# Two more formed heads, even heads moved to ScalarE and VectorE, and attending that reads its high halves first

## The chip, the cores and the metric

The kernel runs on one core of a Trainium2 chip. Its time is the device time of one execution in microseconds; a shown time is the median of several runs. A core has a matrix engine (TensorE, PE), whose weight loads stand apart in the profile as PEld, and VectorE (DVE), ScalarE (ACT) and GpSimd (POOL). SyncE (SP) issues most DMAs. The engines run side by side and meet at semaphores.

## The reference

A block of attention and a mixture of low-rank experts, on x of 2 x 512 tokens of 512 values, in float32. There are 32 heads of 128.

```
x = x + layernorm(attention(layernorm(x)))
x = x + layernorm(ffn(layernorm(x)))

attention(n):
    q = rms_norm(n @ Wq + bq, gq)        # Wq, Wk, Wv: 512 x 4096; rms over all 4096 columns
    k = rms_norm(n @ Wk + bk, gk)
    v = n @ Wv + bv
    per head and batch: softmax(q k^T / sqrt(128)) v
    return concat(heads) @ Wo + bo       # Wo: 4096 x 512

ffn(n):
    base = n @ W_base.T + b_base
    g = softmax(n @ W_gate.T) - sigmoid(n @ W_thr.T + b_thr) / 8, cut at 0 and normed
    return base + 2 * sum over 8 experts e of g[e] * ((n @ A[e].T) @ B[e].T)
```

## The kernel before

**Precision.** A float32 operand is scaled and split into a float16 high half and a float16 low half. A product is three matmuls: high with high, high with low, low with high (lines 1857 to 1859). So every operand is made twice: the high half by ScalarE, the low half (value less high half) by VectorE or GpSimd.

**Stages.** First x is normed, transposed and split (0 to 25 us). Then stage A makes queries and keys of all heads, two heads a pair, 16 pairs, and stores them to a scratch tensor in HBM (to about 340 us). Then stage B attends: for each of 64 steps (16 pairs, 2 heads, 2 batches) the scores, the softmax, its turning by transposing DMAs, the product with the values and that with Wo. Then comes the ffn (from about 1000 us).

**A normal head in stage A** (`phase_a` on each engine) has four items g: query and key of batch 0, query and key of batch 1. An item is 12 matmuls of 128x512 (4 chunks of the contraction, 3 products) into one of eight PSUM banks, 0 to 3 for even heads and 4 to 7 for odd ones. Around it:

- ScalarE: the high halves of the weights of head h + 2, four squares (for the rms sums), and for each query two copies: float32 into `q_s` (line 1272) and the float16 high half into `qk_out` (line 1274).
- VectorE: the factors of head h + 2, the low halves of its weights (line 2550), the largest values of later weights, and the keys (`store_k`, line 2666), each after ScalarE's square of the same bank.
- GpSimd: the low half of each query, `q_s` less its high half (`low_q`, line 824), and adding the squares to `acc` (line 833), 8 additions a pair.
- SyncE: loads of weights, and the stores of a head's query and key, after VectorE's key and GpSimd's low half.

**A formed pair** has a normal even head and a formed odd head. A formed head makes query and key together from 7 products (W_C, W_A, W_E, W_B, W_D, W_G, W_F) of block sums of the weights with block sums of x, in place of 8 block products. Each of the 7 is 6 matmuls of 128x512: 2 chunks, 3 products (lines 1980 to 1982). The even head of a formed pair is already divided in another way: ScalarE makes the high half of the query, then its negated copy in `q_s` from it (line 1396), and the key too (line 1402); VectorE makes the low half from the PSUM bank and `q_s` (line 2799). The weight sums of a formed head are made by GpSimd (`formed_sums`, lines 908 and 913), their high halves by ScalarE (lines 1315, 1318), their low halves by VectorE (lines 2558, 2562). PE's product W_C waits for line 2562.

Pairs 8 to 14 are formed (`FIRST = PAIRS // 2`, `LAST_PAIR = PAIRS - 2`): seven formed heads. The last pair is a normal one.

**Block sums of x.** Four kinds (A, E, D by GpSimd, G by VectorE) are needed once, before the formed pairs. GpSimd's 22 operations on them (sums and low halves, line 850) lie between its additions, at most two kinds for each head of pairs 1 to 7; ScalarE casts the high halves (line 1327).

**Order.** Each engine's order is written out by hand, in the code. Waits are on counts of semaphores. PE's normal heads 2 to 13 are a loop in which the counts come from a register; heads 14 and 15 are written out.

**Attending** (`attend`, line 2090 on): for each of four blocks k three matmuls, value high with turned high, value high with turned low, value low with turned high, after both transposes have landed (lines 717 and 721 issue them, high first). The very last one (lines 2303, 2307) already reads all high halves first, and waits for the low ones after that.

## Time and profile before

| what | value |
|---|---|
| median of 3 runs | 1055.68 us (1052.35 to 1055.7) |
| the profiled execution | 1054.04 us |
| its span | 1052.1 us, 18937 instructions |
| PE busy | 1031.0 us (98%) |
| DVE, ACT, POOL busy | 869.5 (83%), 785.1 (75%), 779.1 us (74%) |

The span is from the first to the last instruction of the profiled execution; 1.9 us lie around it. Busy is the union of an engine's instructions. A matmul's end is modelled, so that matmuls overlap in the record; their starts tell the pace. A wait is named by what ended last before it.

### The profile page before, as it was taken

What the parts mean: (1) busy time and instruction counts of PE and PEld (TensorE: products, weight loads), DVE (VectorE), ACT (ScalarE), POOL (GpSimd) and SP (SyncE); (2) the same over time, 40 slices, a digit from 0 to 9 for tenths busy, and PEclk for the clock granted to TensorE, in tenths of its full rate; (3) what the DMA queues carried; (4) which work ended last, traced back from release to release, by engine and by line L of the source; (5) the groups of instructions that cost most, each with busy time, mean ns of one, the idle gap of its engine ahead of it and who ended that gap; (6) DMA issues with size and microseconds to landing.
All of it is one profiled execution on the core that took longest, in us unless ns stands there. A gap on an engine that the chain in (4) does not pass through costs nothing.

```text
span 1052.1 us, 18937 instructions
## 1 busy us (share of the span) xinstructions
PE 1031.0 (98%) x5607; PEld 544.9 (52%) x5607; DVE 869.5 (83%) x1883; ACT 785.1 (75%) x1618; POOL 779.1 (74%) x717
## 2 busy tenths in 40 slices
PE   7999999999999999999999999999999999999997
PEld 4444444444445655566555555555555555555454
DVE  8988988899886788777887987787887888888887
ACT  4775767777876787776787787788787788778656
POOL 2699999998986568775777877878778778667313
PEclk9999999999999999999999999999999999999999
DMA  6567755666655579958677777867857887886812
GB/s 243 190 228 268 255 201 194 234 243 217 216 189 183 141 190 288 226 134 207 144 194 193 175 181 189 172 171 193 202 161 171 215 192 168 207 200 141 176 36 81
DMA packets 308692, 200.04 MB, mean 190 GB/s; under 512 B 271472, under 2 KB 275440, under 8 KB 308592
## 3 DMA queue, kind: packets, MB, share of 16 engines
q1 hardware_dynamic: 304208, 194.24, 67.0%
q10 hardware_dynamic: 4384, 4.62, 1.6%
q8 instruction: 45, 0.74, 0.3%
q14 instruction: 55, 0.45, 0.1%
HBM read 96.03 MB, written 35.68 MB: 125 GB/s over the span
## 4 chain that ended last, share of the span: by engine, by line
PE 73%; DVE 12%; ACT 7%; issue 4%; DMA 1%; POOL 1%; SPq 1%; ACTq 0%; DVEq 0%; POOLq 0%
PE ps L1857 21%; PE ps L1858 21%; PE ps L1859 21%; PE ps L2120 3%; PE ps L2121 3%; PE ps L2122 3%; DVE pair_q L2960 2%; ACT ps L1537 2%; DVE wa_lo L2550 1%; DVE y L2973 1%; DMA pair_k<-pair_q 1%; ACT pair_q L1546 1%; ACT squares L1265 1%; DVE ps L2946 1%; PE ps L1980 1%
## 5 line engine op out<-in xcount | busy, mean ns | idle before, releaser
L2960 DVE SCALAR_TENSOR_TENSOR pair_q<-ps,row_inv,pair_q 128x512 f16<-128x512 f32 x256 | 174.4, 743 | 47.2 <-ACT pair_q L1546 43.4
L1537 ACT ACTIVATE ps<-ps,neg_max 128x512 f32<-128x512 f32 x256 | 168.3, 657 | 58.2 <-DVE ps L2946 58.2
L2946 DVE TENSOR_SCALAR_CACHE_REDUCE ps<-ps,score_down 128x512 f32<-128x512 f32 x256 | 177.2, 754 | 16.3 <-PE ps L1859 15.6
L1546 ACT ACTIVATE pair_q<-ps,row_inv 128x512 f16<-128x512 f32 x256 | 154.5, 689 | 7.3 <-DVE row_inv L2953 7.1
L1857 PE MATMUL ps<-xh,wa_hi 128*128 128x512 f16 x400 | 151.6, 379 | 1.8 <-DVE wa_lo L2550 1.8
L1859 PE MATMUL ps<-xh,wa_lo 128*128 128x512 f16 x400 | 151.6, 379 | 0.0
L1858 PE MATMUL ps<-xl,wa_hi 128*128 128x512 f16 x400 | 151.6, 379 | 0.0
L1018 POOL TENSOR_TENSOR k_lo<-qk_in,k_hi 128x512 f16<-128x512 f32 x62 | 71.7, 1157 | 39.3 <-ACT k_hi L1494 39.2
L1857 PE MATMUL ps<-wo_hi,oth 128*128 128x512 f16 x256 | 97.1, 379 | 1.2 <-issue 0.9
L1857 PE MATMUL ps<-k_hi,qk_in 128*128 128x512 f16 x256 | 97.1, 379 | 1.0 <-issue 0.7
L1858 PE MATMUL ps<-k_lo,qk_in 128*128 128x512 f16 x256 | 97.0, 379 | 0.0
L1859 PE MATMUL ps<-k_hi,qk_in 128*128 128x512 f16 x256 | 97.0, 379 | 0.0
L1859 PE MATMUL ps<-wo_hi,otl 128*128 128x512 f16 x256 | 97.0, 379 | 0.0
L1858 PE MATMUL ps<-wo_lo,oth 128*128 128x512 f16 x256 | 97.0, 379 | 0.0
L1049 POOL CAST oth<-o_t 128x512 f16<-128x512 f32 x62 | 38.4, 619 | 70.1 <-ACT o_t L1511 70.1
L1265 ACT ACTIVATE squares<-ps,q_k_bias,qk_down 128x512 f32<-128x512 f32 x100 | 77.5, 782 | 15.1 <-PE ps L1859 9.0
L1511 ACT ACTIVATE o_t<-ps,tab 128x512 f32<-128x512 f32 x62 | 42.7, 689 | 60.0 <-PE ps L1859 59.8
L833 POOL TENSOR_TENSOR acc<-acc,squares 128x512 f32<-128x512 f32 x64 | 85.1, 1350 | 0.0
L1012 POOL TENSOR_TENSOR qk_in<-qk_in,rms_row 128x512 f32<-128x512 f32 x62 | 78.9, 1272 | 0.6 <-ACT rms_row L1499 0.6
L924 POOL TENSOR_TENSOR acc<-acc,squares 128x512 f32<-128x512 f32 x56 | 75.0, 1364 | 0.6 <-ACT squares L1265 0.5
L1051 POOL TENSOR_TENSOR otl<-o_t,oth 128x512 f16<-128x512 f32 x62 | 71.6, 1155 | 5.0
L2973 DVE SCALAR_TENSOR_TENSOR y<-ps,y_down,y 128x1024 f32<-128x1024 f32 x55 | 70.1, 1274 | 0.0
(373 smaller groups left out, 2785.3 us busy)
## 6 DMA issues: line engine op xcount, KB each, us to landing
q_k_scratch<-qk_out SPq DMA_DIRECT2D x64, 512.0 KB, 3.0
qk_in<-q_k_scratch SPq DMA_DIRECT2D x64, 512.0 KB, 3.7
wa_stage<-w_qk SPq DMA_DIRECT2D x32, 512.0 KB, 4.4
u_stage<-w_vo SPq DMA_DIRECT2D x32, 512.0 KB, 5.2
wo_stage<-w_vo SPq DMA_DIRECT2D x16, 512.0 KB, 6.4
x_first<-w_vo SPq DMA_DIRECT2D x12, 512.0 KB, 4.6
qk_tops<-qk_top_scratch ACTq DMA_DIRECT2D x27, 128.0 KB, 3.9
pair_k<-pair_q SPq DMA_TRANSPOSE x130, 4.0
```

Of the source, the lines that this page charges most:

```text
L833: pool.tensor_tensor(acc[:, w, cols], acc[:, w, cols], squares[:, par, w, cols], ALU.add).then_inc(acc_ready, 1)
L924: pool.tensor_tensor(part(acc[:, w, :]), part(acc[:, w, :]), part(squares[:, par, w, :]), ALU.add).then_inc(acc_ready, 1)
L1012: pool.tensor_tensor(qk_in[:, s, 0, :], qk_in[:, s, 0, :], factors(b), ALU.mult).then_inc(qk_scaled, 1)
L1265: act.activation(squares[:, par, w, b * S:(b + 1) * S], ps[:, 4 * par + g, :], ACT.Square, bias=q_k_bias[:, par, w:w + 1], scale=qk_down[: ...
L1537: act.activation(ps[:, SCORE + i, :], ps[:, SCORE + i, :], ACT.Exp, bias=neg_max[:, sl, i:i + 1], scale=-1.0, accum_out=row_sum[:, sl, i:i ...
L1546: act.activation(pair_q[:, 0, i, :], ps[:, SCORE + i, :], ACT.Identity, scale=row_inv[:, sl, i:i + 1]).then_inc(high_ready, 1)
L1857: pe.matmul(outp, lhs[0], rhs[0], start=first, stop=False)
L1858: pe.matmul(outp, lhs[0], rhs[1], start=False, stop=False)
L1859: return pe.matmul(outp, lhs[1], rhs[0], start=False, stop=last)
L2946: dve.tensor_scalar(ps[:, SCORE + i, :], ps[:, SCORE + i, :], score_down[:, sl, i:i + 1], None, ALU.mult, ALU.min, accum_out=neg_max[:, sl ...
L2960: dve.scalar_tensor_tensor(out=pair_q[:, 1, i, :], in0=ps[:, SCORE + i, :], scalar=row_inv[:, sl, i:i + 1], in1=pair_q[:, 0, i, :], op0=AL ...
L2973: dve.scalar_tensor_tensor(out=y[:, tiles, :], in0=ps[:, YB:YB + 2, :], scalar=y_down[:, :], in1=y[:, tiles, :], op0=ALU.mult, op1=ALU.add ...
```

## The change

- `FIRST` becomes `PAIRS // 2 - 2`: pairs 6 to 14 are formed, nine formed heads, and pairs 1 to 5 are normal ones of the new kind.
- Even heads of normal pairs 1 to 5 are divided between ScalarE (`even_head`) and VectorE (`even_low`) as in a formed pair; GpSimd's `low_q` goes for them, and SyncE's stores wait for VectorE's low half.
- GpSimd's sums of x go six to a pair into pairs 1, 2 and 3, the rest into 4 and 5.
- PE waits, before an even head writes a query bank, for VectorE's low half of the even head before. PE's loop is written out.
- `attend` runs its 8 matmuls with turned high halves first, and waits for the low transpose only before the other 4.

```diff
-        FIRST, LAST_PAIR = PAIRS // 2, PAIRS - 2
+        FIRST, LAST_PAIR = PAIRS // 2 - 2, PAIRS - 2
...
-        X_FORMS, X_CASTS, Q_LOWS = 22, 8, 2 * FORMED_A
+        X_FORMS, X_CASTS, Q_LOWS = 22, 8, 2 * LAST_PAIR
...
+            def store_even(h, b):
+
+                sp.wait_ge(k_out_ready, 2 * h + 1 + b)
+                sp.wait_ge(k_low_ready, h - 1 + b)
+                sp.dma_start(q_k_scratch[h:h + 1, b].rearrange("a p w n -> p (a w) n"),
+                             qk_out[:, 0, b]).then_inc(stored[0][b], 16)
...
@@ GpSimd
-                        low_q(par, b, 2 * h + b + 1)
+                        if par:
+                            low_q(par, b, 2 * h + b + 1)
...
-            phase_a(1, high_a, low_a)
-            phase_a(2, both_halves)
-            phase_a(3, split_a, high_e)
-            phase_a(4, low_e)
-            phase_a(5, split_e, high_d)
-            phase_a(6, low_d, split_g)
-            for p in range(7, FIRST):
-                if p == FIRST - 1:
-                    formed_sums(2 * FIRST + 1)
-                if p == 7:
-                    phase_a(p, split_d)
-                else:
-                    phase_a(p)
+            phase_a(1, high_a, low_a, both_halves)
+            phase_a(2, split_a, high_e, low_e)
+            phase_a(3, split_e, high_d, low_d)
+            phase_a(4, split_d)
+            formed_sums(2 * FIRST + 1)
+            phase_a(5, split_g)
...
@@ ScalarE
+            def even_head(h, slot, cast):
+
+                for b in range(2):
+                    half = slice(b * S, (b + 1) * S)
+                    act.wait_ge(acc_ready, 4 * h + 2 + 2 * b)
+                    act.wait_ge(stored[0][b], 8 * h)
+                    act.wait_ge(qk_product, 4 * h + 2 * b + 1)
+                    act.activation(pair(qk_out[:, 0, b, 1, :])[:, 0, :], ps[:, 2 * b, :], ACT.Identity,
+                                   bias=q_b[:, slot:slot + 1], scale=Q_DOWN)
+                    square(0, 2 * b, slot, 4 * h + 2 * b + 1)
+                    if b == 0:
+                        load_tops(h + 3, 1)
+                        act.wait_ge(k_out_ready, 2 * h)
+                        act.wait_ge(k_cols_ready, 3 * h + 3)
+                    act.wait_ge(sq_ready, 4 * h + 2 * b + 1)
+                    act.activation(q_s[:, 0, half], pair(qk_out[:, 0, b, 1, :])[:, 0, :], ACT.Identity,
+                                   bias=q_b[:, slot:slot + 1], scale=-1.0).then_inc(q_hi_ready, 1)
+                    square(0, 2 * b + 1, slot, 4 * h + 2 * b + 2)
+                    act.activation(qk_out[:, 0, b, 0, :], ps[:, 2 * b + 1, :], ACT.Identity,
+                                   bias=gain_up[:, h:h + 1], scale=k_g[:, slot:slot + 1]).then_inc(k_out_ready, 1)
+                    if b == 0:
+                        store_tops(h + 4, 0)
+                        if cast is not None:
+                            cast_x(cast, 0)
...
-            casts = {3: XA, 5: XE, 6: XG, 7: XD}
+            casts = {2: XA, 3: XE, 4: XD, 5: XG}
...
@@ TensorE
                 pe.wait_ge(k_out_ready, 2 * h - 3)
+                if par == 0 and h > 2:
+                    pe.wait_ge(k_low_ready, h - 3)
                 q_or_k(par, 0, o % 4)
...
-            with pe.Fori(1, PAIRS // 4) as i:
-                for o in range(-2, 2):
-                    phase_a(i, o)
-            for i, o in NORMAL[14:]:
+            for i, o in NORMAL[2:]:
                 phase_a(i, o)
...
             def attend(n, sl, b, bank=OB, v=(vh, vl)):
                 pe.wait_ge(high_turned, 16 * n + 16)
-                pe.wait_ge(low_turned, 16 * n + 16)
                 d = slice(sl * P, (sl + 1) * P)
                 for k in range(TB):
-                    ins = three(ps[:, bank, :], (v[0][:, TB * b + k, d], v[1][:, TB * b + k, d]),
-                                (pair_k[:, sl, 0, :, k, :], pair_k[:, sl, 1, :, k, :]), k == 0, k == TB - 1)
+                    for half in range(2):
+                        pe.matmul(ps[:, bank, :], v[half][:, TB * b + k, d], pair_k[:, sl, 0, :, k, :],
+                                  start=k == 0 and half == 0, stop=False)
+                pe.wait_ge(low_turned, 16 * n + 16)
+                for k in range(TB):
+                    ins = pe.matmul(ps[:, bank, :], v[0][:, TB * b + k, d], pair_k[:, sl, 1, :, k, :],
+                                    start=False, stop=k == TB - 1)
                 ins.then_inc(o_product, 1)
...
@@ VectorE
+            def even_low(h, b):
+
+                dve.wait_ge(q_hi_ready, 2 * h + 1 + b)
+                dve.scalar_tensor_tensor(out=pair(qk_out[:, 0, b, 1, :])[:, 1, :], in0=ps[:, 2 * b, :],
+                                         scalar=Q_DOWN, in1=q_s[:, 0, b * S:(b + 1) * S], op0=ALU.mult,
+                                         op1=ALU.add).then_inc(k_low_ready, 1)
+
...
                 for b in range(2):
-                    dve.sem_inc(begun, 1)
-                    dve.wait_ge(stored[par][b], 16 * (2 * i + o // 2))
-                    dve.sem_inc(begun, 1)
-                    store_k(par, b, o % 4, 4 * h + 2 * b + 2)
+                    if par:
+                        dve.wait_ge(stored[par][b], 16 * (2 * i + o // 2))
+                        store_k(par, b, o % 4, 4 * h + 2 * b + 2)
+                    else:
+                        even_low(h, b)
```

## Rows read from the trace of the kernel before

**Rows 1.** The page: busy times by engine, PE clock by slice, chain by engine.
```profile
PE 1031.0 (98%) x5607; PEld 544.9 (52%) x5607; DVE 869.5 (83%) x1883; ACT 785.1 (75%) x1618; POOL 779.1 (74%) x717
...
PE 73%; DVE 12%; ACT 7%; issue 4%; DMA 1%; POOL 1%; SPq 1%; ACTq 0%; DVEq 0%; POOLq 0%
```

**Rows 2.** Chain of waits in order of time: start us, us, what.
```profile
789.26 0.22 PE ps L1858
...
968.63 2.04 ACT ps L1537 x6
...
977.61 2.04 ACT ps L1537 x6
...
991.33 6.07 DMA pair_k<-pair_q
```

**Rows 3.** Timeline of PE, product W_C: start us, us, engine line op [idle before].
```profile
205.71 0.38 PE L1980 MATMUL ps<-xh,rms_row 128*128 128x512 f16 x1
...
225.13 0.38 PE L1980 MATMUL ps<-xh,w_form_a 128*128 128x512 f16 x1
...
244.77 0.39 PE L1980 MATMUL ps<-xh,rms_row 128*128 128x512 f16 x1
...
284.39 0.39 PE L1980 MATMUL ps<-xh,rms_row 128*128 128x512 f16 x1
...
303.66 0.38 PE L1859 MATMUL ps<-xh,wa_lo 128*128 128x512 f16 x1
304.37 0.39 PE L1980 MATMUL ps<-xh,w_form_a 128*128 128x512 f16 x1 [0.33 <-DVE w_form_a L2562]
```

**Rows 4.** Table of stretches: stretch, its us, busy us (instructions) by engine, clock, DMA.
```profile
225.13:244.77 19.64, 19.59 (x92) 8.73 (x90) 17.40 (x34) 15.64 (x27) 17.06 (x15) 1.00 0.64 232
...
284.39:304.37 19.98, 19.65 (x91) 8.61 (x91) 17.76 (x34) 15.89 (x27) 17.40 (x15) 1.00 0.55 198
...
59.00:79.70 20.70, 20.70 (x98) 9.39 (x97) 17.96 (x33) 15.09 (x26) 20.62 (x17) 1.00 0.66 228
```

**Rows 5.** Timeline of DVE, key of a formed head and what it waited for.
```profile
286.13 0.81 DVE L2793 TENSOR_SCALAR qk_out<-ps,k_b,k_g 128x512 f32<-128x512 f32 x1 [1.20 <-ACT squares L1373]
```

**Rows 6.** Instructions on `qk_out`: count, duration ns min/median/max, first and last start.
```profile
L824 POOL TENSOR_TENSOR qk_out<-q_s,qk_out x36: 1146/1158/1610, 28.6 to 381.7; 128x512 f16<-128x512 f32 x36
...
L1396 ACT ACTIVATE q_s<-qk_out,q_b x14: 710/712/723, 188.5 to 318.2; 128x512 f32<-128x512 f16 x14
L1402 ACT ACTIVATE qk_out<-ps,gain_up,k_g x14: 762/766/772, 192.4 to 322.2; 128x512 f32<-128x512 f32 x14
L2799 DVE SCALAR_TENSOR_TENSOR qk_out<-ps,q_s x14: 674/678/684, 194.5 to 322.1; 128x512 f16<-128x512 f32 x14
```

**Rows 7.** Timeline of ACT, a cast of a sum of x.
```profile
161.29 0.64 ACT L1327 ACTIVATE xs<-qk_in 128x512 f16<-128x512 f32 x1
```

**Rows 8.** Timelines of POOL (additions of head 3) and ACT (square of head 5).
```profile
64.66 2.95 POOL L833 TENSOR_TENSOR acc<-acc,squares 128x512 f32<-128x512 f32 x2
...
77.70 0.78 ACT L1265 ACTIVATE squares<-ps,q_k_bias,qk_down 128x512 f32<-128x512 f32 x1 [0.46 <-PE ps L1859]
```

**Rows 9.** Timeline of PE before attends, and its row in the list of waits.
```profile
907.58 0.27 PE L2122 MATMUL ps<-w_form_b,xl 128*128 128x256 f16 x1
907.92 0.38 PE L1857 MATMUL ps<-pair_k,v_b 128*128 128x512 f16 x1
...
980.08 0.38 PE L1859 MATMUL ps<-wo_hi,otl 128*128 128x512 f16 x1
980.72 0.38 PE L1857 MATMUL ps<-pair_k,v_b 128*128 128x512 f16 x1 [0.26 <-DMA pair_k<-pair_q]
...
995.20 0.38 PE L1859 MATMUL ps<-wo_hi,otl 128*128 128x512 f16 x1
997.44 0.39 PE L2303 MATMUL ps<-pair_k,v_b 128*128 128x512 f16 x1 [1.86 <-DMA pair_k<-pair_q]
...
PE ps L1857 <- DMA pair_k<-pair_q: 0.8, 3, 0.3
```

More of the change, by code:

```diff
@@ L553, in store_qk, with store_half @@
                              qk_out[:, par, b]).then_inc(stored[par][b], 16)
+            def store_even(h, b):
[3 more added lines that the diff above has]
+                             qk_out[:, 0, b]).then_inc(stored[0][b], 16)
+            def store_half(h, b):
+                if h % 2 == 0:
+                    store_even(h, b)
+                else:
+                    store_qk(h, 1, b, 2 * h + 1 + b, h - 1)
             def phase_a(i, o, weights=True, unit=3, more=None):
@@ L627, in formed_pair @@
                 sp.wait_ge(k_out_ready, 2 * h + 4)
-                sp.wait_ge(q_lo_ready, 4 * FIRST + 2 * f + 2)
+                sp.wait_ge(q_lo_ready, h + 4)
                 for b in range(2):
@@ L895, in split_g @@
             def split_g(c):
-                low_half(XG, two(qk_in[:, 2, c, :]), c, 5 + c)
+                low_half(XG, two(qk_in[:, 2, c, :]), c, 7 + c)
             def split_d(c):
-                low_half(XD, of_first(c), c, 7 + c)
+                low_half(XD, of_first(c), c, 5 + c)
             def formed_sums(h):
@@ L1325, in cast_x @@
                 else:
-                    act.wait_ge(x_formed, {XA: 5, XE: 11, XD: 18}[kind] + c * (2 if kind == XD else 1))
+                    act.wait_ge(x_formed, {XA: 3 + 3 * c, XE: 9 + 3 * c, XD: 15 + 3 * c}[kind])
                 act.activation(xs[:, 0, kind, c, :], qk_in[:, 2 if kind == XG else 0, c, :],
                                ACT.Copy).then_inc(k_high_ready, 1)
+            def even_head(h, slot, cast):
[21 more added lines that the diff above has]
+                            cast_x(cast, 0)
             def phase_a(i, o, formed=False, cast=None):
@@ L1341, in phase_a @@
                 act.wait_ge(q_b_ready, h + 1)
+                if par == 0:
+                    even_head(h, o % 4, cast)
+                    return
                 for g in range(4):
@@ L1944, in phase_a @@
                 pe.wait_ge(k_out_ready, 2 * h - 1)
+                if par == 0 and h > 2:
+                    pe.wait_ge(k_low_ready, h - 2)
                 q_or_k(par, 2, o % 4)
@@ L2677, in _ @@
             dve.wait_ge(k_cols_ready, 6)
+            dve.scalar_tensor_tensor(out=gain_up[:, :], in0=tab[:, 1, :], scalar=X_UP, in1=tab[:, 3, :],
+                                     op0=ALU.mult, op1=ALU.mult)
             first_factors(2)
@@ L2745, in phase_a @@
                         largest_of_unit(h + more, (par + more) % 2, 16 * (2 * i + (o + more) // 2 + 1))
-            phase_a(1, -2, unit=0)
-            phase_a(1, -1, unit=0)
-            phase_a(1, 0, unit=0)
-            phase_a(1, 1, unit=0, more=1)
-            phase_a(2, -2, unit=1, more=2)
             def half_g(half, c, to):
@@ L2760, in both_g @@
                                   ALU.add).then_inc(x_by_dve, 1)
-            dve.wait_ge(xl_ready, NT)
-            half_g(xh, 0, 2)
-            phase_a(2, -1)
-            half_g(xl, 0, 3)
-            phase_a(2, 0)
-            half_g(xh, 1, 2)
-            phase_a(2, 1)
-            half_g(xl, 1, 3)
-            phase_a(3, -2)
-            both_g(0)
-            phase_a(3, -1)
-            both_g(1)
-            dve.scalar_tensor_tensor(out=gain_up[:, :], in0=tab[:, 1, :], scalar=X_UP, in1=tab[:, 3, :],
-                                     op0=ALU.mult, op1=ALU.mult)
-            for h in range(12, 2 * FIRST):
-                phase_a(*NORMAL[h], formed=h == 2 * FIRST - 1)
+            units = {2: (0, None), 3: (0, None), 4: (0, None), 5: (0, 1), 6: (1, 2)}
+            sums_of_g = {4: (half_g, xh, 0, 2), 5: (half_g, xl, 0, 3), 6: (half_g, xh, 1, 2),
+                         7: (half_g, xl, 1, 3), 8: (both_g, 0), 9: (both_g, 1)}
+            for h in range(2, 2 * FIRST):
+                unit, more = units.get(h, (2, None))
+                phase_a(*NORMAL[h], unit=unit, more=more, formed=h == 2 * FIRST - 1)
+                if h == 4:
+                    dve.wait_ge(xl_ready, NT)
+                if h in sums_of_g:
+                    one, *where = sums_of_g[h]
+                    one(*where)
             def formed_pair(p, more=None):
@@ L2794, in formed_key @@
                                       k_g[:, slots[1]:slots[1] + 1], ALU.add, ALU.mult).then_inc(k_out_ready, 1)
-                def even_low(b):
-                    dve.wait_ge(q_hi_ready, 2 * h + 1 + b)
-                    dve.scalar_tensor_tensor(out=pair(qk_out[:, 0, b, 1, :])[:, 1, :], in0=ps[:, 2 * b, :],
-                                             scalar=Q_DOWN, in1=q_s[:, 0, b * S:(b + 1) * S], op0=ALU.mult,
-                                             op1=ALU.add).then_inc(k_low_ready, 1)
                 next_factors(h + 2, 0, (h + 2) % 4)
@@ L2827, in formed_pair @@
                     low_wa(h + 3, (h + 3) % 4)
-                even_low(1)
+                even_low(h, 1)
                 formed_key(1, 8 * p + 8)
```

29 lines of the change are left out of this document (14 added, 15 removed).

## The prediction

> **What bounds the kernel now.** I read the page's busy shares first. TensorE (PE) is busy 98% of the span, every other engine 83% or less, and three quarters of the chain that ended last is PE [rows 1]. The PE clock digits are all 9 (full speed), so no clock is to be won. The reader is to see that only two things shorten this kernel: fewer PE instructions, or a PE idle stretch that goes and whose successor isn't late for another reason.
>
> Next the chain of waits in order of time, to see where that is not so [rows 2]. Up to about 880 us it is matmul after matmul. From there to the last step it is a ring of ScalarE exponentials (ACT), VectorE low halves (DVE) and transposing DMAs: one round from 968.63 to 977.61 is 8.98 us, without PE in it. It ends in a DMA of 6.07 us, for which PE waits before 997.44 [rows 9].
>
> Third, the matmuls in order of time. The page gives a 128x512 matmul 379 ns, but that is latency; what counts is the distance of starts. From the first product of one formed pair to that of the next it is 225.13 - 205.71 = 19.42 us [rows 3], over 90 matmuls (48 of the even head, 42 of the formed head): 0.2158 us each. I read the waits from starts too, since a gap under 0.16 us is hidden in the modelled ends.
>
> **What the change removes on PE.** A normal head is 4 items of 12 matmuls, 48. A formed head is 7 products of 6, 42. FIRST goes from 8 to 6, so pairs 6 and 7 become formed: 2 x 6 x 0.2158 = 2.6 us less PE work. A normal pair takes 96 x 0.2158 = 20.7 us, and the table of stretches shows PE without a gap over such a pair [rows 4].
>
> The Trainium skill ("TensorE: Matmul & The Clock Gate", section Back-to-back issue gap) gives about 131 ns a matmul of 512 columns in a sustained stream; by it the removed work would be an estimated 12 x 0.131 = 1.6 us. The same section's formula for a single one gives 216 ns, and that is what this case's starts show, so the measured 0.2158 is used.
>
> **What a formed pair really costs.** The next starts of that product are 244.77, 284.39 and 304.37 [rows 3]. So periods are 19.42, 19.64, then 39.62 for two, then 19.98 us: 0.2, 0.4 (twice), 0.5 above the 19.42 that PE needs. The later the pair, the more it waits. The wait is in front of this very product: from 303.66 to 304.37 is 0.71 instead of 0.22 us, and the row names DVE line 2562 (low halves of the formed weights). In the period to 304.37 DVE is busy 17.76 us [rows 4] and stands 1.20 us waiting for ACT's square before line 2793 [rows 5]; with some 0.2 us gaps between its small dependent factors it needs about 19.8 to 20 us a pair. DVE enters the formed stage with a lead, PE eats it in two pairs, and after that the DVE/ACT loop sets the pace. None of this loop is edited. So nine formed pairs in a row are two free ones and seven that wait, and the two added ones are of the waiting kind: 20.7 - 19.9 = 0.8 us gained each, **1.6 us** for both, not 2.6. The bounds are 2.6 (the lead lasts, periods 19.42) and 0.5 (the wait keeps growing by some 0.15 a pair, to 20.3 and 20.6: 0.4 + 0.1). I take the value nearest to the last period measured.
>
> **Even heads of pairs 1 to 5: ACT and DVE instead of POOL.** Per even head ACT keeps 4 squares and 2 query copies, swaps 2 for the negated copies (712 ns) and gets 2 keys (766 ns) [rows 6]: +1.6 us a pair. The stretch of a normal pair has ACT busy 15.09 of 20.70 us [rows 4]; it goes to 16.7, and with both casts of x (0.64 each [rows 7]) to at most 18. DVE gives up 2 keys of 0.81 (the same operation as in rows 5) and gets 2 low halves of 0.68: -0.3 us on 17.96. POOL loses 2 low halves of 1.16 [rows 6]. All this hides under the 20.7 us of PE: **0**. Below nothing isn't possible, since PE has no wait there. PE gets two new waits, for the low half of the head before last in the same bank; that was made a whole odd head (10.4 us) earlier, and behind it only PE's own items queue. ACT gets a wait for DVE's keys of the head before, which DVE makes ahead of the factors that ACT has waited for already, so nothing new is late. If this cover fails, what is late is the ring of the rival below. SP's stores of even heads no longer wait for POOL, so the loads queued behind them can only be earlier.
>
> **Sums of x, six a pair.** All 22 sums and splits must be done by pair 6 instead of pair 8. POOL in pair 1 had 4 low halves, 8 additions and 4 sums, 16 operations. Now pairs 1 to 3 have 2 + 8 + 6 = 16 each, pairs 4 and 5 have 12, with four weight sums between. At the pace of 16 in 20.6 us of POOL [rows 4] POOL keeps up with PE in pairs 1 to 3, but catches nothing up, as it could before in pairs 2 and 4 (14 operations). Its reserve: the additions that end at 67.61 free squares that ACT writes next at 77.70 [rows 8], about 10 us. After pair 5 the last split is due only when W_D begins, 60 matmuls or 13 us into pair 6. **0**, with an upper bound in the rival below. The other edits (one small DVE operation moved forward, PE's loop of 12 heads written out, counts of semaphores) have no row that waits for them: 0, at most 0.2 us each.
>
> **Attending reads high halves first.** The same 12 matmuls, with the 4 that read the low halves last, 8 x 0.216 = 1.7 us later. The low transpose is issued after the high one and lands later, so the wait for it shrinks by up to 1.7 us. Where did PE wait there? Four times; of them the first and the last stand in [rows 9]: 907.58 to 907.92 is 0.34 where a half-width matmul needs 0.11, and 980.08 to 980.72 is 0.64 where 0.22 is needed. All four come to 1.5 us by starts. The list of waits has three of them, 0.8 us, since it sees only what lies beyond the modelled ends. All four would go. But all lie after 900 us, where the chain runs through ACT, DVE and DMA [rows 2]. PE gets there sooner and then stands longer for the last transposes (995.20 + 0.22 to 997.44 is 2.0 us now; 3.5 then). I take 0.2 us of the 1.5, since the transposes wait for the attend before; bounds 0 and 1.5.
>
> **Sum.** 1.6 + 0 + 0 + 0.2 = 1.8 us. The profiled execution took 1054.04 us (span 1052.1 and 1.94 around it), 1.64 below the median shown, 1055.68, in runs from 1052.35. From the profile the sum gives 1052.2, from the median 1053.9; I name the middle, **1053.1 us**. A difference of 0.3% (3.2 us) is about what a measurement of this kernel can tell from no change, and the sum is 0.17%.
>
> **Rivals.**
> - Everything counts: DVE's lead lasts, so 2.6 us, and the ring behind 900 us is PE's after all, so 1.5 more. 4.1 us, 1050.8 from the same middle. For it: the first two periods of formed pairs are free, and some waits in the ring are near PE's own step. Against it: the growth of the wait, and 8.98 us of ring without PE. Chance 0.22.
> - The formed stage is worse: each later pair waits more, 20.3 and 20.6 us, gain 0.5 us, and the attend edit brings 0: 1054.4. For it the rising series. Against it: DVE's own work stays 17.4 to 17.8 us a pair. Chance 0.20.
> - Slower: POOL falls behind in pairs 1 to 3. Place: the additions that free the squares. The low halves take from 1.15 to 1.61 us [rows 6]; if all 16 took 1.60, a pair would be 25.6 us, 4.9 over PE's 20.7, 14.7 after three pairs, less 10 of reserve: 4.7 us on PE, net 2.9 slower, 1057.8. It decides from a mean of 1.50 us an operation (24 us a pair, 3.3 over, three times). The mean now is 20.62 / 16 = 1.29 [rows 4]. Chance 0.10. The Trainium skill ("SBUF — State Buffer", section SBUF: two separate sides) names a port pair that DVE operations with two SBUF inputs and GpSimd operations hold exclusively; here DVE's new low half reads PSUM and one SBUF input, so by that rule it would not add to it. No run here shows it.
> - That the change does not do what it says: the formed pairs count 9 but the waits move before the first of them. That is in the ranges above.
>
> **Numbers.** Forecast 0.48. Faster by over 0.3%: nearly all of the first rival and the upper edge of the forecast, 0.27. Slower: the last rival, 0.10. Same 0.63. The range reaches from just below the first rival, 1050.0, to 1056.5, short of the slow rival.
>
> **What would show it.** Right: matmuls fall by 12; formed pairs from about 142 us on (the first now begins at 205.71 - 102 x 0.2158 = 183.7, less two normal pairs of 20.7); periods 19.4, 19.4, then 19.6 to 20.0, total wait near 2.5 us; no PE wait in 38 to 142 us; POOL full until about 120 us; no wait before an attend, but a longer one before the last attend, line 2303 now. Wrong: a PE wait in pairs 1 to 5, periods that stay 19.42, or a last wait that does not grow.

## The result and the profile after

| | median us (runs) | profiled run, us | span | granted clock |
|---|---|---|---|---|
| before | 1053.08 (6) | 1054.04 | 1052.1 | 0.999 |
| after | 1057.92 (6) | 1056.82 | 1055.0 | 0.997 |

After / before is 1.004, with 0.9983 forecast; the 95% interval is 1.0027 to 1.0053. The change made the kernel slower by 4.2 us by that ratio (0.4%; the two medians differ by 4.8), and 1057.92 lies outside the range on record. One execution of e5 (3883.57 us) and one of e7 (2819.38 us) below were far slower than all others, and the ratios go by the fast runs alone. The two profiled runs differ by less, 2.8 us. The forecast of 1053.1 also started too high, since the three runs first shown (median 1055.68) lay above the later ones (1053.1 to 1053.7 in every set). By ratio it is off by 0.6%.

The page of the kernel after, the rows that answer to [rows 1]:

```profile
PE 1030.4 (98%) x5595; PEld 543.7 (52%) x5595; DVE 885.6 (84%) x1889; ACT 798.8 (76%) x1636; POOL 770.7 (73%) x711
...
PE 63%; DVE 15%; ACT 12%; issue 6%; DMA 2%; POOL 1%; ACTq 1%; SPq 1%; DVEq 0%; POOLq 0%
```

The busy shares say almost nothing: the 12 matmuls are gone, POOL is less busy, PE still at 98%. The chain says more: PE's part fell from 73% to 63%, and DVE, ACT and issue took it over. The view that settles it is the timeline of PE where the chain leaves PE (start us, us, engine line op, idle before and its releaser):

```profile
144.81 0.38 PE L1895 MATMUL ps<-xh,wa_lo 128*128 128x512 f16 x1
148.30 0.48 PE L2016 MATMUL ps<-xh,w_form_a 128*128 128x512 f16 x1 [3.12 <-DVE qk_out L2704]
148.57 0.63 PE L2017 MATMUL ps<-xl,w_form_a 128*128 128x512 f16 x1
149.00 0.63 PE L2018 MATMUL ps<-xh,w_form_a 128*128 128x512 f16 x1
...
151.56 0.53 PE L2018 MATMUL ps<-xs,wa_lo 128*128 128x512 f16 x1
151.93 0.38 PE L2016 MATMUL ps<-xs,wa_hi 128*128 128x512 f16 x1
```

From 144.81 to 148.30 is 3.49 us, where a matmul needs 0.22: a wait of 3.3 us in front of product W_C of the first formed pair. In this pair alone the code waits there for VectorE's first key of head 11 (batch 0). Behind it the starts are 0.43 apart until 151.56, twice 0.216. The table of stretches for these two windows (PEclk is the number behind POOL's count):

```profile
148.30:151.80 3.50, 3.50 (x9) 1.31 (x10) 2.29 (x5) 3.37 (x7) 3.50 (x4) 0.52 0.37 150
151.80:155.30 3.50, 3.50 (x17) 1.57 (x16) 3.08 (x10) 3.15 (x6) 3.50 (x4) 0.99 0.79 219
```

The granted clock is 0.52, the 1.2 GHz level, right behind the stand, then 0.99. Nine matmuls start in the first window and 17 in the second; by starts the nine took 1.7 us longer than at the upper level. (Whether these 1.7 us are a price of their own is looked at under e5.) The Trainium skill ("TensorE: Matmul & The Clock Gate", section Wait — 56ns, not 53.3ns?) gives starts of 426.7 ns at 1.2 GHz and 215.7 ns at 2.4 GHz for 512 columns; the trace agrees with both (0.43, 0.216).

Stage A, up to the first column sum, ends 2.9 us later: in before it starts at 334.22, in after here:

```profile
337.13 1.84 PE L2070 MATMUL ps<-ones,acc 128*128 128x1 f32 x16
```

The account by distances of starts: -2.6 (12 matmuls) + 3.3 + 1.7 + 0.4 (waits before later W_C and smaller ones, 2.0 in all against 1.6) + 0.2 (first 25 us) = 3.0, against the 2.9 read off. Two executions of the same code up to this point can differ too: e1 and e9 below, which change nothing in stage A, end it at 334.88 and 335.33. The rest of the span changes little in the profiled runs: from there to the start of the last matmul of the last attend (stage B) it is 665.6 us in before and 665.1 in after, behind it 52.3 and 52.8. Inside stage B something is hidden all the same, at the one backward branch of its loop. ACT and PE there, after:

```profile
682.99 0.69 ACT L1547 ACTIVATE o_t<-ps,tab 128x512 f32<-128x512 f32 x1 [2.25 <-issue]
```
```profile
683.00 0.39 PE L1893 MATMUL ps<-k_hi,qk_in 128*128 128x512 f16 x1 [1.38 <-issue]
```

("issue" is time in which the engine waited for nothing that the profile shows), and in before, where ACT waits for PE at that place and not for "issue":

```profile
679.00 0.39 PE L1857 MATMUL ps<-k_hi,qk_in 128*128 128x512 f16 x1 [0.70 <-issue]
```

### The profile page after: what moved, and what is told of

Its sections match the earlier page's. It is cut to its first block, busy times and chain, and to the rows that moved or that the text cites. A ratio compares the mean times of both kernels' runs of the same rounds, so it can differ in the third digit from the quotient of the medians.

```text
span 1055.0 us, 18786 instructions
## 1 busy us (share of the span) xinstructions
PE 1030.4 (98%) x5595; PEld 543.7 (52%) x5595; DVE 885.6 (84%) x1889; ACT 798.8 (76%) x1636; POOL 770.7 (73%) x711
## 4 chain that ended last, share of the span: by engine, by line
PE 63%; DVE 15%; ACT 12%; issue 6%; DMA 2%; POOL 1%; ACTq 1%; SPq 1%; DVEq 0%; POOLq 0%
PE ps L1893 13%; PE ps L1895 12%; PE ps L1894 12%; PE ps L2129 9%; PE ps L2133 4%; PE ps L2158 3%; PE ps L2160 3%; PE ps L2159 3%; ACT squares L1273 3%; ACT ps L1573 2%; DVE pair_q L2992 2%; DVE wa_lo L2588 2%; ACT wa_hi L1240 2%; DMA pair_k<-pair_q 1%; PE ps L2016 1%
## 5 line engine op out<-in xcount | busy, mean ns | idle before, releaser
L1893 PE MATMUL ps<-xh,wa_hi 128*128 128x512 f16 x368 | 139.5, 379 | 1.8 <-DVE wa_lo L2588 1.8
L1895 PE MATMUL ps<-xh,wa_lo 128*128 128x512 f16 x368 | 139.5, 379 | 0.0
L1894 PE MATMUL ps<-xl,wa_hi 128*128 128x512 f16 x368 | 139.5, 379 | 0.0
L1273 ACT ACTIVATE squares<-ps,q_k_bias,qk_down 128x512 f32<-128x512 f32 x92 | 71.3, 777 | 8.5 <-PE ps L1895 5.4
```

The source lines that it names most:

```text
L1273: act.activation(squares[:, par, w, b * S:(b + 1) * S], ps[:, 4 * par + g, :], ACT.Square, bias=q_k_bias[:, par, w:w + 1], scale=qk_down[: ...
L1893: pe.matmul(outp, lhs[0], rhs[0], start=first, stop=False)
L1894: pe.matmul(outp, lhs[0], rhs[1], start=False, stop=False)
L1895: return pe.matmul(outp, lhs[1], rhs[0], start=False, stop=last)
```

## Why the wait is there: a ring, not a sum

What ends the wait is DVE's first key of head 11 at 147.34; it waited for ACT's square at 146.42, and this for ACT's start into the head. ACT, after:

```profile
139.87 0.77 ACT L1356 ACTIVATE qk_out<-ps,gain_up,k_g 128x512 f32<-128x512 f32 x1
142.16 0.72 ACT L1323 ACTIVATE wa_hi<-wa_stage,qk_up 128x512 f16<-128x512 f32 x1 [1.53 <-DVE qk_up L2529]
...
146.42 0.79 ACT L1273 ACTIVATE squares<-ps,q_k_bias,qk_down 128x512 f32<-128x512 f32 x1
```

DVE, after:

```profile
139.33 0.69 DVE L2769 SCALAR_TENSOR_TENSOR qk_out<-ps,q_s 128x512 f16<-128x512 f32 x1 [1.35 <-ACT q_s L1353]
...
140.82 1.11 DVE L2571 TENSOR_SCALAR qk_down<-qk_most 128x2 f32<-128x2 f32 x1
141.97 0.17 DVE L2529 RECIPROCAL qk_up<-qk_down 128x2 f32<-128x2 f32 x1
...
147.34 0.81 DVE L2704 TENSOR_SCALAR qk_out<-ps,k_b,k_g 128x512 f32<-128x512 f32 x1 [0.90 <-ACT squares L1273]
```

ACT can't begin the weights of head h + 2 before DVE has their factors; DVE gets to the factors only behind its last key or low half of the head before; and that waits for ACT's squares and copies. Both engines stand in turns, each for the other: from 37.22 to 142.16 us ACT is busy 71% and DVE 85%, and where each waits for the other the ring still has no slack. In this ring the start of head 13's weights is at 142.16, where before had 135.81: 6.4 us later, while PE comes only 0.2 later. Against before ACT's starts were 1.8 us late at 37 us, 2.1 at 65, 4.7 at 100 and 6.4 at 142. Three places feed this.

1. At the start. The moved `gain_up` (in before it took 1.25 us behind head 11, at 145.47) and a pair of low weights that now takes 2.27 us (1.37 before) put ACT's first start in the ring at 37.22 instead of 35.38. DVE, after:

```profile
29.17 0.84 DVE L2716 SCALAR_TENSOR_TENSOR gain_up<-tab 128x32 f32<-128x32 f32 x1
...
34.52 2.27 DVE L2588 SCALAR_TENSOR_TENSOR wa_lo<-wa_stage,qk_up,wa_hi 128x512 f16<-128x512 f32 x2
```

2. Heads 5 and 6. DVE's six operations for kind G of the block sums of x (tile XG) stand behind the last key or low half of heads 4 to 9, where before had them at the same place of heads 6 to 11. With the second `largest_of_unit` they now share heads 5 and 6; in before they shared only head 6. DVE and, in the second fence, ACT, after:

```profile
84.03 1.21 DVE L2712 TENSOR_REDUCE vo_top<-u_stage 128x1 f32<-128x1024 f32 x1
85.15 1.69 DVE L2798 TENSOR_TENSOR qk_in<-xl 128x512 f32<-128x512 f16 x1
...
96.22 1.21 DVE L2712 TENSOR_REDUCE vo_top<-u_stage 128x1 f32<-128x1024 f32 x1
97.35 1.57 DVE L2798 TENSOR_TENSOR qk_in<-xh 128x512 f32<-128x512 f16 x1
```
```profile
75.77 1.33 ACT L1240 ACTIVATE wa_hi<-wa_stage,qk_up 128x512 f16<-128x512 f32 x2 [1.27 <-DVE qk_up L2529]
87.83 1.33 ACT L1240 ACTIVATE wa_hi<-wa_stage,qk_up 128x512 f16<-128x512 f32 x2 [4.64 <-DVE qk_up L2529]
99.90 1.34 ACT L1240 ACTIVATE wa_hi<-wa_stage,qk_up 128x512 f16<-128x512 f32 x2 [2.99 <-DVE qk_up L2529]
```

ACT's starts are 12.06 and 12.07 us apart there, a head of PE is 10.4. In before the ring was over PE's pace at this place too, but less, 11.2 and 11.1 us (72.81, 84.02, 95.16), so each of the two heads adds 0.9 us to the lag:

```profile
84.02 1.34 ACT L1232 ACTIVATE wa_hi<-wa_stage,qk_up 128x512 f16<-128x512 f32 x2 [2.95 <-DVE qk_up L2491]
95.16 1.33 ACT L1232 ACTIVATE wa_hi<-wa_stage,qk_up 128x512 f16<-128x512 f32 x2 [3.69 <-DVE qk_up L2491]
```

3. The cast of x (0.64 us), now in each of heads 4 to 11; before had only four of the eight by 142 us.

The shares of the three were not taken apart.

PE doesn't feel the lag in normal heads: they need the key of the head before only with their third item, 24 matmuls in. The first formed pair asks for it 12 matmuls in, and begins at head 12 instead of 16.

## The experiments

Every run was timed in five rounds beside the kernel before, whose medians were 1053.74 (e1 to e4), 1053.18 (e5 to e8), 1053.12 (e9 to e11) and 1053.43 (e12). Changes are told by ratio.

| run | median us (runs) | ratio to before, 95% | stage A ends | stage B |
|---|---|---|---|---|
| e1 attend alone | 1053.92 (11) | 1.0001 (0.9992 to 1.0011) | 334.88 | 664.5 |
| e2 formed from pair 8 | 1056.80 (8) | 1.0029 (1.0018 to 1.0039) | 332.94 | 669.3 |
| e3 XG sums beside | 1053.28 (11) | 0.9999 (0.9990 to 1.0008) | 332.88 | 666.1 |
| e4 key item first | 1057.28 (5) | 1.0041 (1.0027 to 1.0055) | 337.10 | 666.1 |
| e5 after, loop written out | 1054.66 (11) | 1.0020 (1.0009 to 1.0031) | 337.41 | 663.6 |
| e6 e2, loop written out | 1050.51 (11) | 0.9974 (0.9965 to 0.9983) | 333.44 | 662.3 |
| e7 e3 and casts earlier | 1053.41 (11) | 1.0006 (0.9996 to 1.0016) | 333.57 | 665.2 |
| e8 e7, loop written out | 1050.35 (11) | 0.9976 (0.9967 to 0.9985) | 334.28 | 663.0 |
| e9 before, loop written out | 1053.08 (11) | 0.9999 (0.9990 to 1.0008) | 335.33 | 665.5 |
| e10 e3, loop written out | 1051.60 (11) | 0.9976 (0.9961 to 0.9991) | 333.11 | 663.2 |
| e11 e6 with XG sums beside | 1051.36 (11) | 0.9982 (0.9972 to 0.9992) | 332.77 | 662.9 |
| e12 e2 and 16 idle instructions | 1051.88 (12) | 0.9983 (0.9973 to 0.9993) | 332.84 | 664.3 |

**e1: the kernel before with the new order of attending alone.**

```diff
                 pe.wait_ge(high_turned, 16 * n + 16)
-                pe.wait_ge(low_turned, 16 * n + 16)
...
+                pe.wait_ge(low_turned, 16 * n + 16)
```

The rest of the edit is the order of the twelve matmuls, as in the change.

> The kernel before with only the new order in attend. Ring theory (the time is lost in stage A, before the first formed head): the four waits before attends go (1.5 us in the trace of before), the wait for the last transposes grows by as much, the time is that of before within 1 us. Rival, the new attend costs something by itself (more PE waits or a later ring of ACT and DVE in stage B): slower by 1 to 3 us. Rival of my forecast's upper side: faster by 1.5 us.

1.0001: the attend edit brings nothing and costs nothing that can be told.

**e2: the changed kernel, formed pairs from pair 8 on.** As before the change, seven formed heads.

```diff
-        FIRST, LAST_PAIR = PAIRS // 2 - 2, PAIRS - 2
+        FIRST, LAST_PAIR = PAIRS // 2 - 0, PAIRS - 2
```

GpSimd's part gets the two further normal pairs, with the weight sums ahead of the last one.

> The changed kernel with pairs 8 to 14 formed as before (seven formed heads); even heads of pairs 1 to 7 divided in the new way, sums of x six a pair, new attend. Ring theory: ACT and DVE are as late at head 11 as in the changed kernel (ACT begins the weights of head 13 near 142 us), but have two pairs without casts and sums of x to catch up, so no PE wait before the first product W_C and no fall of the clock; 1052 to 1054 us, as before. Rival, the new division of even heads or the sums of x cost PE time by themselves: a PE wait between 38 and 184 us, slower by 2 us or more. Rival, GpSimd is late: it is busy without a gap up to 142 us and ACT waits for acc.

The wait before the first formed pair is gone, and so are the small ones in front of the later W_C (0.1 us in all by starts). ACT's lag near 142 us is as in after (141.17 for head 13), so it takes both to make PE stand: the lag, and a formed stage that begins before it is made up. Stage A ends at 332.94, 1.3 us ahead of before, with 12 matmuls more than after. The time missed what I expected (1052 to 1054): it was hardly better than after, since stage B is 4.2 us longer than in after, 3.7 longer than in before. DVE of e2 at the loop's branch:

```profile
680.02 0.76 DVE L2983 TENSOR_SCALAR_CACHE_REDUCE ps<-ps,score_down 128x512 f32<-128x512 f32 x1
684.61 0.08 DVE L2983 DVE_READ_ACCUMULATOR ps<-ps,score_down 128x1 f32 x1 [3.83 <-issue]
```

```profile
683.97 0.38 PE L1900 MATMUL ps<-wo_hi,otl 128*128 128x512 f16 x1
687.89 0.28 PE L2163 MATMUL ps<-w_form_b,xh 128*128 128x256 f16 x1 [3.54 <-ACT ps L1601]
...
688.55 0.42 PE L2164 MATMUL ps<-w_form_b,xh 128*128 128x256 f16 x1
688.77 0.42 PE L2165 MATMUL ps<-w_form_b,xl 128*128 128x256 f16 x1
```

DVE stands in the middle of its own row of instructions, waiting for no semaphore that the profile shows. This was the first sign of a second cause.

**e3: the sums for XG moved off the ring**, behind the first unit of the head instead of behind its last key or low half (shortened):

```diff
                     if b == 0:
                         largest_of_unit(h + unit, ...)
+                        if h in sums_of_g:
+                            one(*where)
...
-                if h in sums_of_g:
-                    one(*where)
```

> The changed kernel with VectorE's six operations for the sums of kind G moved from the end of heads 4 to 9 (between its last key or low half and the factors of head h + 2, for which ScalarE waits) to the middle of the same head (after the first largest_of_unit), where it waits 1.0 to 1.8 us for ScalarE. Same work. Ring theory: each such head is 1 to 1.5 us shorter in the ring, ScalarE begins the weights of head 13 at 137 to 139 us instead of 142.2, the PE wait of 3.3 us before the first W_C goes or falls below 1 us, the clock keeps its upper level, gain 3.5 to 5 us against the changed kernel: 1053 to 1054.5. Rival, VectorE's total of work binds and not its order: nothing changes, 1058. Rival, the wait comes from the weight sums (GpSimd, ScalarE line 1326) and not from the keys of head 11: nothing changes.

Stage A of e3 against after, PE in front of the first formed pair and at the column sum:

```profile
144.85 0.38 PE L1895 MATMUL ps<-xh,wa_lo 128*128 128x512 f16 x1
145.06 0.38 PE L2016 MATMUL ps<-xh,w_form_a 128*128 128x512 f16 x1
...
332.88 1.84 PE L2070 MATMUL ps<-ones,acc 128*128 128x1 f32 x16
```

No wait, no fall of the clock, ACT's start of head 13's weights at 136.84 instead of 142.16, stage A 4.2 us shorter than in after and 1.3 shorter than in before. The same six operations, done on the same engine at another place in its order, win back the whole loss of stage A. It is not DVE's total of work: from 75.5 to 99.6 us DVE is busy 22.21 us here, and in after from 75.77 to 99.90 only 20.95. Since before had the six at the end of heads too, only two heads later, this shows how the time is lost, and not that they alone made the lag.

**e4: the first formed pair's key item put in front of W_C.**

```diff
                 q_or_k(0, 0, slots[0])
+                if f == 0:
+                    q_or_k(0, 1, slots[0])
                 pe.wait_ge(wa_lo_ready, 2 * h + 4)
```

The item's old place goes for this pair, and two of ACT's counts follow the new order.

> The changed kernel with one reorder in the first formed pair alone: PE does the key of batch 0 of the even head (12 matmuls, 2.6 us) before product W_C. Ring theory: the PE wait is 3.3 - 2.6 = 0.7 us and stands before W_C as before, the clock does not fall, gain 4 us: 1053.5 to 1054.5. Rival, PE's wait is for something that comes after PE's own order (a buffer that the later items free): the wait stays 3 us. Rival, the clock falls for another reason than the wait: the half pace stays, gain 2.6 us.

A miss of my expectation: W_C starts at 148.29 as in after, and 2.6 us of other work ahead of it only moved the wait behind W_A, in front of W_E, with the fall of the clock behind that. PE of e4:

```profile
148.29 0.38 PE L2016 MATMUL ps<-xh,w_form_a 128*128 128x512 f16 x1 [0.53 <-DVE qk_out L2707]
...
153.90 0.59 PE L2016 MATMUL ps<-xs,w_form_a 128*128 128x512 f16 x1 [2.86 <-ACT ps L1405]
```

ACT's copy L1405, for which W_E waits, starts at 153.17, and at 153.18 in after, where PE comes to W_E only later. So it is ACT as a whole that is late, not one key, and of the two cures only e3's is one.

**e5: the changed kernel with stage B's loop written out** on all five engines.

```diff
-            with pe.Fori(1, FORMED // 2) as i:
+            for i in range(1, FORMED // 2):
```

> The changed kernel with the loop of stage B written out on all five engines (its one backward branch lies near 680 us; there the profile has ScalarE stand 2.2 us and PE 1.4 us for nothing that it shows). Same work and order. Theory that part of the loss is this branch, whose price depends on where the change has moved the code: stage A ends at 337.1 us as before, the stands near 680 us go, stage B is 0.6 to 1.5 us shorter, 1056.5 to 1057.3. Rival, the stands are waits on other engines that the profile doesn't name: they stay. Rival, more code costs fetches: slower.

The stands at the branch are gone, the 3.3 us before the first formed pair stay (145.10 to 148.61). 1.0020 against 1.0040: about 2 us are the branch's, by ratios whose intervals just overlap (1.0009 to 1.0031, 1.0027 to 1.0053). By the profiles it is 1.5 us of stage B. All eight profiled kernels with the loop have PE stand for "issue" there, 0.54 to 0.81 us in before, e1, e2 and e12, and 1.34 to 1.88 in after, e3, e4 and e7, where ACT also stands 2.1 to 2.6. None of the six with the loop written out has such a stand there.

This run also tells what the fall of the clock was worth. Behind the same stand of 3.3 us the clock stayed at its upper level (a row of PE's timeline and the same stretch as above, both of e5):

```profile
148.61 0.38 PE L2016 MATMUL ps<-xh,w_form_a 128*128 128x512 f16 x1 [3.12 <-DVE qk_out L2704]
...
148.30:151.80 3.50, 3.19 (x15) 1.49 (x16) 2.42 (x4) 3.47 (x7) 3.50 (x4) 1.00 0.37 150
```

But stage A is no shorter. From the matmul behind the last transposes of x (25.61 us in after, 25.89 here) to the column sum it is 311.52 us in both. PE came sooner and stood instead: 0.4 us for ACT's copy L1405 at 154.21, and 0.2, 0.3 and 0.6 before the next three W_C, where after has next to nothing. So the end of stage A was set by DVE and ACT, and the 1.7 us of the lower clock in after lie where PE would have waited anyway.

**e6: e2 with the loop written out.**

> The kernel of e2_eight_first (pairs 8 to 14 formed) with stage B's loop written out. In e2 VectorE stood 3.8 us at 680.8 us for nothing shown, PE waited 3.5 us after it, and the clock was at its lower level for some 4 us. Branch theory: all of it goes, 3.7 + 2 = 5.7 us less, 1051 us, the fastest so far, with no PE wait in stage A. Rival, the new division or the six sums a pair cost the 3 us of e2 by themselves: 1056 to 1057.

0.9974, as the branch theory says: no PE wait in stage A, no stand at the branch, and stage B is 662.3 us, 7.0 less than in e2.

**e7: e3, and the casts of x moved to the start of a head on ACT.**

```diff
                 h, par = 4 * i + o, o % 2
+                if cast is not None:
+                    cast_x(cast, par)
```

> e3_g_beside and with it ScalarE's eight casts of the sums of x moved from the middle of a head to its start, ahead of the high halves of weights, where ScalarE waits 1.3 to 3.3 us for VectorE's factors. Ring theory: each head with a cast is up to 0.5 us shorter in the ring, ScalarE begins the weights of head 13 at 133 to 135 us (142.2 in the changed kernel, 136.8 in e3), no PE wait before the first W_C, and stage A ends no later than in e3 (332.9 us). 1052 to 1053.5, as stage B decides. Rival, ScalarE's work is the bound and not its place in the ring: as e3, 136.8.

1.0006 against e3's 0.9999, and ACT starts the weights of head 13 at 136.93, as the rival says: the place of the casts doesn't matter.

**e8: e7 with the loop written out.**

> e7 with the loop of stage B written out. Both theories: stage A as in e7 (332.9 us or earlier), stage B without the stand at the branch, 664.5 us or less: 1050.5 to 1051.5 us, 2 to 3 us under the kernel before and the fastest of all. If the end of stage B is set by the ring of ScalarE, VectorE and transposes alone, only 1 us of it shows: 1052.

0.9976, with stage B at 663.0 us: as expected.

**e9: the kernel before with the loop written out**, the control for e5, e6, e8 and e10.

> The kernel before with the loop of stage B written out on all engines, nothing else. It tells how much of the 2.5 to 3 us that the two written-out versions of nine heads and of eight gained over the kernel before is only the loop's branch. Theory (the branch has a price that hangs on the layout of the code, and the kernel before pays the smallest one seen: its profile shows PE standing only 0.70 us near the branch, where the others show PE 1.4 to 3.7 and ACT or DVE 2.2 to 3.8): faster by 1 to 1.5 us, 1051.7 to 1052.3 against 1053.2, stage B 664.1 to 664.6 instead of 665.1. Then the change with its sums beside the ring and the loop written out (1050.4) keeps 1.3 to 1.9 us of its own, near the 1.6 of the prediction. Rival: the branch costs the kernel before as much as the others (3 us), 1050.3, and the whole gain of those versions is the branch, none the change's. Second rival: written-out code of this length costs something by itself (fetching), no gain.

Theory and first rival missed: 0.9999, the second rival's number. Whether the kernel before pays nothing at the branch, or written-out code costs as much as the branch saves, this run can't tell (its profile has no stand at the branch, but waits of 1.6 and 0.7 us at 517 and 527 us, for a transpose and for ACT, where the other profiles have none and at most 0.5; and the execution profiled was the slowest of the eleven). The 665.1 us that the text on record gives for stage B of the kernel before are those of after; before has 665.6, and e9 665.5. Either way it is the control: what e6, e8 and e10 have over it is the change's own and not the loop's. The branch cost after about 2 us and e2 about 6 (1.0029 to 0.9974).

**e10: e3 with the loop written out.**

> The changed kernel with the sums of gates moved off the ring of ScalarE and VectorE (as in the run with only that edit, 1053.3) and the loop of stage B written out. The casts stay at their place. Theory: both causes are gone at once, and they add: 1053.3 less the branch (3.3 us in the changed kernel, 6.3 in the one of eight heads; stage B should come to 662.3 to 663.6 from 666.1), so 1050.0 to 1050.8, as the version that also moves the casts (1050.4). Rival: the casts' place has a price that the branch hid, and this one is 0.5 to 1 us behind, 1051.1 or more.

0.9976, the same as e8 by ratio. By the medians of its set it is 0.9986, and its 1051.60 lies in the range of the rival; the interval (0.9961 to 0.9991) holds both, so the two theories are not told apart.

**e11: e6 with the XG sums beside the ring.** The text on record calls this eight formed heads; FIRST is pair 8 as in e2, so there are seven.

> As the run before it in this call, but with eight formed-or-later start (FIRST back at 8 heads' pairs less one: eight formed heads instead of nine), sums of gates beside the ring, loop written out. It tells what the ninth formed head is worth once both causes are gone. By the periods of the prediction a further formed pair that waits brings 0.8 us. Theory: with one formed pair less, the formed stage begins later, VectorE's lead is as large and PE does not wait in it, so the formed head that is left out costs nothing on the clock: equal to the nine-head version within 0.5 us, 1050.0 to 1050.8. Rival: the ninth head brings its 6 matmuls and more, 1.3 us, and this one is at 1051.5.

0.9982 with seven formed heads, 0.9976 with nine: the two heads on which the forecast counted 1.6 us bring at most a few tenths, and the intervals overlap. Table of stretches, PE busy first, of e11 and then of e10 over their formed pairs:

```profile
184.00:303.00 119.00, 119.00 (x554) 53.93 (x552) 103.48 (x200) 95.38 (x155) 99.30 (x83) 1.00 0.62 214
```
```profile
203.80:303.10 99.30, 98.32 (x451) 43.17 (x450) 88.62 (x166) 79.90 (x132) 87.33 (x71) 1.00 0.63 220
```

With seven PE never stands, with nine it stands 1.0 us beyond the modelled ends (2.4 us by starts), which takes back nearly all of the 2.6 us of matmuls. This is as the theory on record has it.

**e12: e2 with 16 semaphore additions on DVE in front of its loop**, which nobody waits for.

```diff
+            for _ in range(16):
+                dve.sem_inc(begun, 1)
             with dve.Fori(1, FORMED // 2) as i:
```

> The version with seven formed heads (formed pairs from pair 8 on, as before the change) and the loop of stage B kept, plus 16 semaphore additions that nobody waits for, on VectorE alone, just ahead of its loop. Without them this version took 1056.8 (1.0029 times the kernel before), and its VectorE stands 3.83 us near 684 us at the loop's branch, with TensorE 3.7 behind it. Theory (the price hangs on where the loop's code lies, not on what the code does): VectorE's stand changes by more than 1 us, to 0 to 2.5, stage B falls from 669.3 to 664 to 667, and the time to 0.998 to 1.001 of the kernel before, 1051 to 1054. ScalarE or TensorE may show a stand of its own, 1 to 2.5, that lay under VectorE's. Rival: the stand belongs to the work at that place (the same loop in all versions, entered with this version's order of the buffers), the shift of code does nothing, VectorE 3.8 again and 1056.8. Second rival: the position within the code decides, but 16 instructions are a whole number of its blocks, and nothing changes; then this run can't tell it from the first rival.

From 1.0029 to 0.9983, 4.9 us faster by 16 instructions that do nothing. DVE of e12 at the place where e2 stood 3.83 us:

```profile
680.64 0.76 DVE L2983 TENSOR_SCALAR_CACHE_REDUCE ps<-ps,score_down 128x512 f32<-128x512 f32 x1
681.31 0.14 DVE L2983 DVE_READ_ACCUMULATOR ps<-ps,score_down 128x1 f32 x1
```

Neither the loop nor its work differ from e2, only where DVE's code lies. The additions themselves cost nothing: DVE's rows ahead of them (512.88 us) and behind them (521.84) are both 0.2 us later than in e2. Of e2's stands there only PE's own is left (0.81 us). So the price at the branch hangs on where the code lies; one shift on one engine was tried. What moves there can be seen in the DMA queues of the stretch 675 to 690 us (packets, MB, share), here of after; before, e2 and e12 have seven or eight such packets there too, e5 has none, e6 one and e9 two:

```profile
q8 instruction: 3, 0.05, 1.8%
q14 instruction: 5, 0.04, 0.8%
```

The Trainium skill ("Runtime: NRT & Kernel Launch", section Instruction fetch mechanics) says that a taken branch whose target isn't in the small window of code at hand stops the engine until it is fetched, and that code comes in blocks of 256 instructions. The traces agree with the first: stands and seven or eight packets of code at the branch in the looped kernels, no stand and at most two packets without it. The block size no run here shows.

## Why the prediction was wrong, step by step

- **Matmuls, 12 fewer, 0.2158 us each: right.** 5607 to 5595.
- **Formed pairs, -1.6 us for two more: right in size against the kernel before, wrong in why they wait.** In e3, where the lag is gone, PE's starts lose 2.7 us in stage A against 1.6 in before; with 2.6 us of matmuls less that is a gain of 1.5. The periods there are 19.4 twice, 20.1 once and then 19.8, with no growth from pair to pair (in after 21.1 with the lower clock, 19.4 twice, then 19.8). But the wait is not a property of formed pairs: with seven of them and the new division of even heads none waits (e2, e6, e11), so e10 against e11 puts the worth of the two further heads at nearly nothing.
- **Even heads by ACT and DVE with sums of x done sooner, 0: in this part it was better than that.** With seven formed heads the new early stage frees the formed pairs of all waits: e2, e6 and e11 end stage A 1.3, 1.9 and 2.6 us ahead of before with the same kind of loop, of which up to about 1 us can be the spread of single profiles. Which of the two edits does it was not taken apart.
- **"All this hides under the 20.7 us of PE", with sums of x at 0: this is the step that failed.** I added busy times of ACT and DVE in a pair and compared them with PE's 20.7. The busy times did stay below (DVE 18.1 us in a pair at 69 to 89.7 us of after). But the two wait for each other in a ring, and in heads 5 and 6 it took 12.1 us a head, not 10.4. Of DVE's own sums of kind G, which the change moves two heads forward, the prediction says nothing; its paragraph on sums of x prices GpSimd's alone. The row of ACT waiting for `qk_up` (1.8 to 4.5 us in most heads) stood in the trace of before; I had read it as slack. The lag cost a stand of 3.3 us at the first formed pair, and stage A ended 4.2 us later than in e3, which took all of it back by moving six operations. I named the ring for the even heads ("what is late is the ring of the rival below") but priced only POOL's.
- **The slower rival: right that it could go slower, and near in size (1057.8) by luck, since its place is wrong.** POOL fell behind nowhere; its one wait from 100 to 145 us was 2.57 us for ACT, at 125.28. The real place was DVE and ACT.
- **The other edits, "0, at most 0.2 us each": wrong.** `gain_up` moved forward takes 0.84 us in the ring (its share of the lag was not tried alone). And the branch of stage B's loop, over 500 us later, became about 2 us dearer, by e5, in a kernel whose code has moved; that a shift of code can do this is shown on DVE by e12, for ACT's stand in after it is not tried.
- **Attending, -0.2: the number holds within what can be told, the way to it does not.** e1 shows 1.0001. The waits before attends went, as forecast. But the wait before the last attend was to grow from 2.0 to 3.5 us; in after it shrank to 0.3, with 0.4 more in front of its last four matmuls. PE stands elsewhere instead, 1.1 us for POOL at 990.03 and 0.6 at 946.01, where before had 0.4 and 0.2. A last wait that does not grow was one of my signs of being wrong.

e10 is 2.5 us faster than before by ratio (0.9976), 1.5 by the medians of its set, and so near the 1.8 that were forecast, but that is luck: e6, with seven formed heads, gains as much (0.9974). The gain comes with edits that I had put at 0. e6, e8, e10, e11 and e12 all beat both kernels, and the intervals don't tell them apart; e12 does it with the loop kept.

## What to carry to other kernels

Where two engines feed each other in turns, don't add busy times under the bound engine: follow one round (who starts, on what, behind which instruction) and ask of each operation that moves whether it stands before or behind the one that the partner waits for. A consumer that begins to ask earlier in its order (12 matmuls in, not 24) turns a lag that was free into a wait. When a version is off by a few us at a loop's branch, shift the code by a few idle instructions or write the loop out before believing anything about the edit. And a slower clock behind a stand is not a loss of its own where another engine sets the end: compare with a run that has the same stand without it.

## Not expected of the hardware

- 16 idle instructions on one engine were worth 4.9 us (e2 to e12): the stand at a backward branch went from 3.83 us on DVE to nothing there.
- A stand of PE of 3.0 to 3.7 us was followed by about 3 us at the lower clock in after, e4 and e2 (0.50 to 0.53), but one of 3.3 us in e5 was not (1.00).
- `gain_up` on 128x32 took 0.84 us in after and 1.25 in before, where another operation on 128x32 just ahead of it took 0.19; the pair of low weights took from 1.37 to 3.18 us at different times, and the first four sums for XG from 0.97 to 1.69 us in after. What stretched them was not tried, and it lengthens the ring.
